# One GNN layer on one core: thirteen blocks of dense work for eight, a gap in the first comparisons, x turned through two banks

## The chip, the cores and the metric

The kernel runs on 1 core of one Trainium2 chip. The metric is the device time of one execution in microseconds, lower is better. Below, PE is TensorE (PEld its weight loads), DVE is VectorE, ACT is ScalarE, POOL is GpSimd and SP is SyncE, whose queue issues most of the DMAs.

## What is computed

A graph with 3125 nodes and 53125 edges sorted by destination, 128 values per node and edge:

```python
msg = x[src] + edge_attr
neigh = segment_sum(msg, dst, num_segments=3125)
rst = (1.0 + eps[0]) * x + neigh
h = rst @ W1 + b1                          # 128 -> 256
h = (h - mean(h, 0)) * rsqrt(var(h, 0) + 1e-5) * gamma + beta
out = relu(h) @ W2 + b2                    # 256 -> 128
y = layernorm(x + out)
```

## The kernel before

The edges are cut into 208 groups of 256. One group is worked on in one window w of the loop in the PE program (L872); window and group order differ. All sums are kept turned, one column of `aggT` per node. Since the edges are sorted by destination, a group touches at most 20 neighbouring nodes.

Every group needs its edge rows summed. `edge_sum` (L837) multiplies the 256 rows, in two halves, with a 0/1 table of 20 columns, in f32; the result goes to one of three banks and DVE adds it into `aggT` (L1214). The rows x[src] come in by one of two ways:

- Gathered groups (50 before). POOL issues two indirect DMAs (L560) that add x[src] to the edge rows already in a slot of `egat`. There are `SLOTS` slots; SP loads a slot's edge rows when the group that used it has been summed (L491).
- Counted groups (158 before, the first 158 in node order). PE counts, with f16 0/1 tables, how often each source node occurs for each of the 20 destinations: `counts_a` (L859, L862) and `counts_b` (L868), 700 columns in all. ACT copies the counts into the f16 matrix `cnt` (L665). DVE makes the tables with comparisons: `hits_k` for two groups at a time (L1125, L1128, L1134), `hits_c` and `hits_g` (L1100) and `hits_n` (L1145). Later the dense work `multiply` (L829) multiplies x with `cnt`.

For the dense work x is split exactly into three bf16 parts, in `xN`, `xr` and `x3` (printed as x_room). `cnt` is cut along the nodes into blocks, `BLOCKS_C` gives the counted groups of each. A block takes 25 tiles of x times 3 parts = 75 units, each a weight load of 128x128 and a matmul whose width is the number of nodes of the block. The widths (`SIZES`) are 120, 180, 256, 376, 468, 466, 332 and 218. The units of block f are spread evenly over the windows between READY[f], when its counts are complete, and READY[f+1] (`share`, L110): the first unit of all is in w = 13, and the last block's 75 units run after the last window. In a counted window, half of the units stand ahead of the first `edge_sum` and half behind `counts_b`; in a gathered window half stand ahead of each `edge_sum`. When a block is done DVE adds it (`add_block`, L1168).

In the windows before and around the first dense unit, called the head here, other work is spread by hand through tables of window numbers:

- SP loads x in seven pieces of 512 nodes in the order of `X_ORDER`: 0, 4, 1, 5, 2, 6, 3. Three are issued ahead of the loop, the others after the windows of `X_AT`.
- `turn_x` turns a piece with four transposes (L773) in a window of `TURN_AT` and ACT scales it into `aggT` (L627). All pieces go through one bank, `ACC`, so a piece waits until the one before it is scaled. The first dense unit waits for all seven.
- The bf16 parts of four pieces are made by DVE (`rest` L1153, `part_3` L1161, windows `SPLITS_W`), those of the other three by PE and ACT: `sum_rest` (L787, L789), windows `RESTS_W`, and `sum_last` (L796) two windows later, through bank `ACC + 1`.
- `fill` (L723) puts matmuls without use ahead of the counts: two for m < 6, one for m < 14.

What of a group goes where is decided when the program is built: `arrange` (L118) walks over the windows with a cost for each and places the gathered groups evenly in that time. PE may be at most three windows ahead of the adds (L877), and DVE makes its tables in the same stream as the adds.

After the last block PE multiplies with W1, DVE takes the statistics, ACT and DVE normalise, PE multiplies with W2 and the rows are normalised and written. The change doesn't touch this part.

Of the kernel before, what the change touches and what calls it, by code (L numbers as in the profile page):

```python
# [5 lines left out]
ALU = mybir.AluOpType  # L6
ACT = mybir.ActivationFunctionType
# [6 lines left out]
P = 128  # L14
BANK = 512
# [5 lines left out]
WIN_A = 12  # L21
FROM_B = 5
WIN_B = 15
GROUPS_C = 158
BLOCKS_C = (10, 12, 17, 25, 31, 31, 22, 10)
CHUNK = 2
CHUNKS = 4
SLOTS = 7
BATCH = 4
BATCHES = 3  # L30
CARRY = 8
# [10 lines left out]
LOADS = 16  # L42
PAD = 8192
PARTS = 3
X_LEAD = 2
SLOTS_W = (0, 2, 5, 7, 10, 13)
SPLITS_W = (3, 6, 10, 14)
RESTS_W = (3, 8, 15)
LATE = 14
BATCHES_G = 2  # L50
KEEP = 0
# [14 lines left out]
FILL_CARRY = 4
FILLS = ((6, 2), (14, 1))
LOAD_0 = 4

def gnn_layer(nc, x, src, dst, edge, eps, w1, b1, gamma, beta, w2, b2, out):
# [6 lines left out]
    NB = -(-N // BANK)  # L78
# [20 lines left out]
    KEYS_A = NT * WIN_A  # L99
# [56 lines left out]
    def width(b):  # L156
        return min(BANK, N - b * BANK)
# [7 lines left out]
    with ExitStack() as ctx:  # L165
# [3 lines left out]
        def sem(name):  # L169
            return ctx.enter_context(nc.semaphore(name))  # L170
# [45 lines left out]
        xN = sb("xN", [P, NT, D])  # L216
# [177 lines left out]
        early_g = columns_of(GC)[0]  # L394
        X_ORDER = [0] + [b for i in range(NB) for b in (early_g + i, 1 + i) if (b < NB if b >= early_g else b == 1 + i)]
        X_ORDER = list(dict.fromkeys(X_ORDER))
        X_AT = [2 + X_LEAD * i for i in range(NB - 3)]
        SLOT_AT = list(SLOTS_W)
        CHUNK_AT = [max(CHUNK * (c - CHUNKS) + CHUNK - 1, min(CHUNK * (c - 2), c + 1)) for c in range(2, GC // CHUNK)]
        W_WEIGHTS = 40  # L400
        assert len(SLOT_AT) == SLOTS - 1 and len(set(CHUNK_AT)) == len(CHUNK_AT)
        SUM_B = [early_g, early_g + 1, early_g - 1]
        SPLIT_B = [b for b in range(NB) if b not in SUM_B]
        SPLIT_AT = list(SPLITS_W)
        REST_AT = list(RESTS_W)
        LAST_AT = [w + 2 for w in REST_AT]
        TURN_AT = [2 * i for i in range(NB)]

        def store_of(w):

# [13 lines left out]
        CLAMP_G = min(GC - GC % LOADS + 3 * LOADS, G)  # L424
        W_CLAMP = 4
        W_CLAMPS = READY[0] + 12
        assert G_AT[0] > 3 and W_CLAMP < G_AT[0] + LAG and W_CLAMPS < min(C_AT[2 * LOADS], G_AT[CLAMP_G - GC])
        W_TESTS = READY[0] + 8
        TEST_F = next(f for f in range(1, F) if READY[f] + 5 > W_TESTS + 8 * TEST_STEP)
        W_WORST = READY[TEST_F] + 5  # L430
# [162 lines left out]
        def _(act):  # L593
# [26 lines left out]
            nc.scalar.activation(carry[:, :].rearrange("p (q h) -> p q h", h=2),  # L620
                                 ps[:, 1, 0:GC].rearrange("p (h q) -> p q h", q=QC), ACT.Copy).then_inc(carry_made, 1)

            def scale_x(i, turned, scaled, bank):

                b = X_ORDER[i]
                act.wait_ge(turned, i + 1)
                nc.scalar.activation(aggT[:, b * BANK:b * BANK + width(b)], bank[:, 0:width(b)], ACT.Copy,  # L627
                                     scale=b2e[:, D:D + 1]).then_inc(scaled, 1)

            def store(made, stored):  # L630
# [8 lines left out]
            for m in range(GC):  # L639
                if m == load_from(m):  # L640
                    act.wait_ge(lows_made, 2 if m < 2 * LOADS else 6)
                    n = load_to(m) - m
                    regs = [act.alloc_register(f"first_act{m + i}") for i in range(n)]
                    act.load(regs, firsts[0:1, m:m + n])
                    lows = [nc.snap(r, donate=True, min_val=0, max_val=CNT - WIN) for r in regs]
                for i in range(len(SUM_B)):
                    t0, t1 = pieces(SUM_B[i])
                    if store_of(REST_AT[i]) == m:
                        act.wait_ge(x_rest_summed, i + 1)
                        nc.scalar.activation(xr[:, t0:t1, :], ps[:, ACC + 1, :].rearrange("p (t d) -> p t d", d=D),  # L650
                                             ACT.Copy).then_inc(x_rest_stored, 1)
                    if store_of(LAST_AT[i]) == m:
                        act.wait_ge(x_last_summed, i + 1)
                        nc.scalar.activation(x3[:, t0:t1, :], ps[:, ACC + 1, :].rearrange("p (t d) -> p t d", d=D),
                                             ACT.Copy).then_inc(x_last_stored, 1)
                for i in range(NB):
                    if store_of(TURN_AT[i]) == m and C_AT[m] > TURN_AT[i]:
                        scale_x(i, x_turned, x_scaled, ps[:, ACC, :])
                act.wait_ge(counts_made, m + 1)
                if m == CORNER:  # L660
                    act.wait_ge(spare_zeroed, 1)
                    act.wait_ge(worst_found, 2)
                if m > 0:
                    act.wait_ge(counts_stored, m)
                nc.scalar.activation(cnt[:, :, bass.ds(lows[m - load_from(m)], WIN)],  # L665
                                     ps[:, m % BANKS_C, 0:KEYS].rearrange("p (t n) -> p t n", n=WIN),
                                     ACT.Copy).then_inc(counts_stored, 1)
                for i in range(NB):
                    if C_AT[m] == TURN_AT[i]:
                        scale_x(i, x_turned, x_scaled, ps[:, ACC, :])  # L670

            act.wait_ge(weights_loaded, 80)
            act.wait_ge(path_known, 1)
# [3 lines left out]
            with act.Else():  # L677
                store(hidden_made, hidden_stored)
                for i in range(NB):
                    scale_x(i, gen_x_turned, gen_x_scaled, ps[:, ACC + i % 2, :])  # L680
                store(gen_hidden_made, gen_hidden_stored)
            act.wait_ge(hidden_moments_made, HH)
            nc.scalar.activation(sd[:, :], bag[:, :, 1], ACT.Sqrt, bias=epsc[:, 0:1]).then_inc(deviation_made, 1)
# [34 lines left out]
        def _(pe):  # L718
# [42 lines left out]
            def turn_x(i, half):  # L761

                b = X_ORDER[i]
                t0, t1 = pieces(b)
                if half == 0:
                    pe.wait_ge(x_loaded[b], 16)
                    pe.wait_ge(key_made, 1)
                    if i > 0:
                        pe.wait_ge(x_scaled, i)
                for t in range(t0 + 2 * half, min(t0 + 2 * half + 2, t1)):  # L770
                    r = rows_of(t)
                    k = (t - t0) * P
                    last = nc.tensor.transpose(ps[:, ACC, k:k + r], xN[0:r, t, :], ident[0:r, 0:r])  # L773
                    if t == t1 - 1:
                        last.then_inc(x_turned, 1)

            def sum_rest(i):

                b = SUM_B[i]
                t0, t1 = pieces(b)  # L780
                pe.wait_ge(x_loaded[b], 16)
                if i == 0:
                    pe.wait_ge(lo_made, 1)
                    pe.wait_ge(minus_made, 1)
                if i > 0:
                    pe.wait_ge(x_last_stored, i)
                nc.tensor.matmul(ps[:, ACC + 1, :], ident[:, :], xN[:, t0:t1, :].rearrange("p t d -> p (t d)"),  # L787
                                 start=True, stop=False, skip_group_check=True)
                nc.tensor.matmul(ps[:, ACC + 1, :].rearrange("p (t d) -> p t d", d=D), minus, upper(xN[:, t0:t1, :]),  # L789
                                 start=False, stop=False, skip_group_check=True).then_inc(x_rest_summed, 1)  # L790
# [212 lines left out]
        def _(dve):  # L1003
# [111 lines left out]
            def hits_k(m):  # L1115

                r = m % RING_K
                if m >= RING_K:
                    dve.wait_ge(counts_made, m - RING_K + 3)

                def pairs(v):
                    return v.rearrange("p (n two) -> p n two", two=2)

                keys = key[:, 2 * m:2 * m + 4, :].rearrange("p (g j) two -> p g j two", j=ROWS)
                nc.vector.tensor_tensor(hit_k[:, r:r + 2, 0:KEYS_A].rearrange("p g (n two) -> p g n two", two=2),  # L1125
                                        pairs(iota_k[:, 0:KEYS_A]).unsqueeze(1).to_broadcast([P, 2, KEYS_A // 2, 2]),
                                        keys[:, :, 0, :].unsqueeze(2).to_broadcast([P, 2, KEYS_A // 2, 2]), ALU.is_equal)
                nc.vector.tensor_tensor(hit_k[:, r:r + 2, KEYS_A:KEYS_A + KEYS_E].rearrange("p g (n two) -> p g n two", two=2),  # L1128
                                        pairs(iota_b[:, :]).unsqueeze(1).to_broadcast([P, 2, KEYS_E // 2, 2]),
                                        keys[:, :, 1, :].unsqueeze(2).to_broadcast([P, 2, KEYS_E // 2, 2]),  # L1130
                                        ALU.is_equal)
                if m == 0:
                    dve.wait_ge(lo_made, 1)
                nc.vector.tensor_tensor(hit_l[:, r:r + 2, :, :].rearrange("p g j (n two) -> p (g j) n two", two=2),  # L1134
                                        pairs(iota_k[:, 0:P]).unsqueeze(1).to_broadcast([P, 2 * ROWS, P // 2, 2]),
                                        lo[:, 2 * m:2 * m + 4, :].unsqueeze(2).to_broadcast([P, 2 * ROWS, P // 2, 2]),
                                        ALU.is_equal).then_inc(key_hits_made, 2)
# [262 lines left out]
```

## Time and profile before

| | |
|---|---|
| median of 3 runs | 258.77 us (257.50 to 259.24) |
| the profiled execution: time | 256.72 us |
| the profiled execution: span of the core | 254.9 us |
| PE busy | 239.1 us (94%), 2147 instructions |
| DVE busy | 182.7 us (72%) |
| POOL busy | 178.7 us (70%) |
| ACT busy | 132.2 us (52%) |

The time holds 1.8 us beside the span. "Busy" is the time in which at least one instruction of the engine ran. PE's matmuls overlap, so its starts tell more than its busy time.

### The profile page before, as it was taken

To read this page: it belongs to the slowest core of one execution; us is meant where nothing else is said; L and a number is where in the kernel's file an instruction comes from. 1 tells how busy PE (TensorE), PEld (TensorE's weight loads), DVE (VectorE), ACT (ScalarE), POOL (GpSimd) and SP (SyncE) were. 2 spreads that over 40 slices of the span, in tenths; PEclk is the share of its full clock that TensorE was granted. 3 is DMA by queue.
4 is the path that set the end of the run, shared out by engine and by line. 5 is a ranking of instruction groups with operands and counts; after the bars stand their busy time and mean duration, and the time that the engine had idled before them with its cause. 6 is when DMAs were issued, how large, how long until landed. Compare 5 with 4: busy or idle time off the path is not lost.

```text
span 254.9 us, 6747 instructions
## 1 busy us (share of the span) xinstructions
PE 239.1 (94%) x2147; PEld 197.8 (78%) x2150; DVE 182.7 (72%) x683; ACT 132.2 (52%) x235; POOL 178.7 (70%) x116
## 2 busy tenths in 40 slices
PE   7997799999999998999999999999999999999970
PEld 3775579989989977888878888888888889645960
DVE  5995757989888867888778687876667311378872
ACT  3365655646556553655554554444443330376793
POOL 4498888888888888888888888888888860550000
PEclk9999999999999999999999999999999999999995
DMA  3868987889988796898787788877756330000044
GB/s 67 236 172 188 230 194 169 186 166 216 208 207 180 193 206 154 194 192 206 180 172 183 191 174 184 180 163 169 169 119 156 74 39 3 0 0 3 3 126 130
DMA packets 51342, 38.13 MB, mean 150 GB/s; under 512 B 5099, under 2 KB 51099, under 8 KB 51305
## 3 DMA queue, kind: packets, MB, share of 16 engines
q1 hardware_dynamic: 36663, 30.89, 43.1%
q0 software_dynamic: 14400, 6.56, 21.5%
q8 instruction: 20, 0.33, 0.6%
q10 hardware_dynamic: 242, 0.21, 0.3%
q14 instruction: 17, 0.14, 0.2%
HBM read 36.05 MB, written 1.60 MB: 148 GB/s over the span
## 4 chain that ended last, share of the span: by engine, by line
PE 83%; DMA 6%; ACT 3%; DVE 3%; issue 2%; POOL 1%; ACTq 1%; another core or an unknown queue 0%; SPq 0%; DVEq 0%; POOLq 0%
PE ps L829 30%; PE ps L837 22%; PE ps L868 11%; PE ps L862 8%; PE ps L806 4%; DMA egat<-in_x_dram,srci 4%; PE ps L948 4%; PE ps L934 2%; PE ps L859 2%; DMA big<-in_src_dram 1%; ACT big L707 1%; DMA egat<-in_edge_attr_dram 1%; ACT big L665 1%; POOL egat L560 1%; ACT aggT L627 1%
## 5 line engine op out<-in xcount | busy, mean ns | idle before, releaser
L560 POOL DMA_INDIRECT egat<-in_x_dram,srci x100 | 168.8, 1688 | 36.4 <-issue 29.0
L665 ACT ACTIVATE big<-ps 128x500 f32 x158 | 96.4, 610 | 92.7 <-PE ps L868 62.7
L837 PEld LDWEIGHTS ps<-hit_c,ebuf 128*128 128x128 f32 x632 | 99.5, 188 | 9.6 <-DVE aggT L1214 2.9
L837 PE MATMUL ps<-hit_c,ebuf 128*128 128x20 f32 x632 | 94.6, 227 | 1.3 <-DVE aggT L1214 1.2
L1214 DVE TENSOR_TENSOR aggT<-aggT,ps 128x20 f32 x208 | 35.9, 173 | 51.1 <-PE ps L837 34.4
L829 PE MATMUL ps<-big,xN 128*128 128x120 f16 (+7 forms) x200 | 58.0, 292 | 1.1 <-ACT aggT L627 0.9
L829 PE MATMUL ps<-big,xr 128*128 128x120 f16 (+7 forms) x200 | 58.0, 292 | 0.0
L829 PE MATMUL ps<-big,x_room 128*128 128x120 f16 (+7 forms) x200 | 57.9, 292 | 0.0
L868 PE MATMUL ps<-hit_k,hit_l 128*128 128x375 f16 x158 | 53.6, 339 | 0.0
L862 PE MATMUL ps<-hit_k,hit_l 128*128 128x300 f16 x158 | 45.5, 288 | 0.0
L1128 DVE TENSOR_TENSOR hit_k<-iota_b,key 128x752 f16<-128x752 f16 x79 | 42.9, 543 | 0.0
L1125 DVE TENSOR_TENSOR hit_k<-iota_k,key 128x600 f16<-128x600 f16 x79 | 36.8, 466 | 0.0
L837 PEld LDWEIGHTS ps<-hit_g,egat 128*128 128x128 f32 x200 | 32.0, 189 | 5.2 <-issue 2.2
L1134 DVE TENSOR_TENSOR hit_l<-iota_k,lo 128x512 f16<-128x512 f16 x79 | 33.0, 417 | 0.0
L837 PE MATMUL ps<-hit_g,egat 128*128 128x20 f32 x200 | 29.5, 229 | 1.7 <-DMA egat<-in_x_dram,srci 1.7
L859 PE MATMUL ps<-hit_n,hit_l 128*128 128x25 f16 x157 | 28.8, 184 | 0.0
L868 PEld LDWEIGHTS ps<-hit_k,hit_l 128*128 128x128 f16 x158 | 28.3, 179 | 0.0
L859 PEld LDWEIGHTS ps<-hit_n,hit_l 128*128 128x128 f16 x157 | 27.3, 174 | 0.7
L829 PEld LDWEIGHTS ps<-big,xN 128*128 128x128 bf16 x200 | 22.2, 111 | 6.7 <-issue 1.7
L829 PEld LDWEIGHTS ps<-big,x_room 128*128 128x128 bf16 x200 | 22.5, 112 | 4.0
L829 PEld LDWEIGHTS ps<-big,xr 128*128 128x128 bf16 x200 | 22.0, 110 | 4.0
L862 PEld LDWEIGHTS ps<-hit_k,hit_l 128*128 128x128 f16 x158 | 15.1, 96 | 0.9
(120 smaller groups left out, 206.5 us busy)
## 6 DMA issues: line engine op xcount, KB each, us to landing
ebuf<-in_edge_attr_dram SPq DMA_DIRECT2D x79, 256.0 KB
egat<-in_edge_attr_dram SPq DMA_DIRECT2D x49, 128.0 KB
egat<-in_x_dram,srci POOLq DMA_INDIRECT x100
xN<-in_x_dram SPq DMA_DIRECT2D x6, 256.0 KB, 4.3
out_dram<-big SPq DMA_DIRECT2D x5, 256.0 KB
w_sb<-in_L_gnn_W_dram SPq DMA_DIRECT2D x2, 128.0 KB
out_dram<-big SPq DMA_DIRECT2D x2, 128.0 KB
big<-in_src_dram ACTq DMA_DIRECT2D x1, 192.0 KB
```

The lines of the kernel that those rows point to most:

```text
L560: return nc.gpsimd.indirect_dma_start(to, None, x[:, :], bass.IndirectOffsetOnAxis(ap=ix, axis=0), compute_op=op)
L665: nc.scalar.activation(cnt[:, :, bass.ds(lows[m - load_from(m)], WIN)], ps[:, m % BANKS_C, 0:KEYS].rearrange("p (t n) -> p t n", n=WIN), A ...
L806: nc.tensor.matmul(ps[:, n % BANKS_C, 0:width(b)], w1_sb[:, h * P:(h + 1) * P], aggT[:, b * BANK:b * BANK + width(b)], start=True, stop=Tr ...
L829: last = nc.tensor.matmul(ps[:, ACC + f % 2, 0:SIZES[f]], part_v, cnt[:, t, STARTS[f]:STARTS[f] + SIZES[f]], start=(u == 0), stop=(u == UN ...
L837: last = nc.tensor.matmul(ps[:, SUMS + w % BANKS_S, 0:WIN], rows_v[:, j * D:(j + 1) * D], hits_v, start=(j == 0), stop=(j == ROWS - 1))
L859: nc.tensor.matmul(counted(m)[:, :, 0], hit_l[:, (m - 1) % RING_K, 1, :], hit_n[:, (m - 1) // CARRY % 2, (m - 1) % CARRY, :], start=True, ...
L862: nc.tensor.matmul(counted(m)[:, :, 0:WIN_A], hit_l[:, m % RING_K, 0, :], hit_k[:, m % RING_K, 0:KEYS_A].rearrange("p (t n) -> p t n", n=W ...
L868: nc.tensor.matmul(counted(m)[:, :, FROM_B:WIN], hit_l[:, m % RING_K, 1, :], hit_k[:, m % RING_K, KEYS_A:KEYS_A + KEYS_B].rearrange("p (t ...
L1125: nc.vector.tensor_tensor(hit_k[:, r:r + 2, 0:KEYS_A].rearrange("p g (n two) -> p g n two", two=2), pairs(iota_k[:, 0:KEYS_A]).unsqueeze(1 ...
L1128: nc.vector.tensor_tensor(hit_k[:, r:r + 2, KEYS_A:KEYS_A + KEYS_E].rearrange("p g (n two) -> p g n two", two=2), pairs(iota_b[:, :]).unsq ...
L1134: nc.vector.tensor_tensor(hit_l[:, r:r + 2, :, :].rearrange("p g j (n two) -> p (g j) n two", two=2), pairs(iota_k[:, 0:P]).unsqueeze(1).t ...
L1214: nc.vector.tensor_tensor(to, to, ps[:, SUMS + v % BANKS_S, 0:WIN], ALU.add).then_inc(window_added, 1)
```

## The change

There are 13 blocks in place of 8, with widths 120, 150, 166, 180, 182, 196, 194, 212, 210, 212, 210, 196 and 218. So there are 975 units in place of 600, the last 75 as before at the width 218 behind the last window. 160 groups are counted and 48 gathered. There are six slots for gathered rows in place of seven. x is turned alternately through the banks `ACC` and `ACC + 1`, in windows that follow more closely, and its pieces are loaded one window earlier or more. `sum_rest` starts later and takes the pieces in the order 3, 4, 5. DVE's `rest` moves by two or three windows. The fillers end at m = 10. In the first seven `hits_k`, the second comparison waits for the first one's semaphore.

```diff
-GROUPS_C = 158
-BLOCKS_C = (10, 12, 17, 25, 31, 31, 22, 10)
+GROUPS_C = 160
+BLOCKS_C = (10, 10, 11, 12, 12, 13, 13, 14, 14, 14, 14, 13, 10)
...
-SLOTS = 7
+SLOTS = 6
...
-SLOTS_W = (0, 2, 5, 7, 10, 13)
-SPLITS_W = (3, 6, 10, 14)
-RESTS_W = (3, 8, 15)
+SLOTS_W = (0, 2, 5, 7, 10)
+SPLITS_W = (5, 8, 12, 17)
+RESTS_W = (9, 12, 15)
+TURNS_W = (0, 2, 3, 5, 7, 8, 10)
+PORT = 14
...
-HITS = 3200
+HITS = 3000
...
-GATHER_FIRST = 19000
+GATHER_FIRST = 18000
...
-FILLS = ((6, 2), (14, 1))
+FILLS = ((4, 2), (10, 1))
...
-        X_AT = [2 + X_LEAD * i for i in range(NB - 3)]
+        X_AT = [1 + X_LEAD * i for i in range(NB - 3)]
...
-        SUM_B = [early_g, early_g + 1, early_g - 1]
+        SUM_B = [early_g - 1, early_g, early_g + 1]
...
-        TURN_AT = [2 * i for i in range(NB)]
+        TURN_AT = list(TURNS_W)
+        BEFORE_SUMS = max(i for i in range(NB) if i % 2 == 1) + 1
...
                 if half == 0:
                     pe.wait_ge(x_loaded[b], 16)
-                    pe.wait_ge(key_made, 1)
-                    if i > 0:
-                        pe.wait_ge(x_scaled, i)
+                    if i == 0:
+                        pe.wait_ge(key_made, 1)
+                    if i == 1:
+                        pe.wait_ge(lo_made, 1)
+                    if i > 1:
+                        pe.wait_ge(x_scaled, i - 1)
...
-                    last = nc.tensor.transpose(ps[:, ACC, k:k + r], xN[0:r, t, :], ident[0:r, 0:r])
+                    last = nc.tensor.transpose(ps[:, ACC + i % 2, k:k + r], xN[0:r, t, :], ident[0:r, 0:r])
...
                 if i == 0:
-                    pe.wait_ge(lo_made, 1)
                     pe.wait_ge(minus_made, 1)
+                    pe.wait_ge(x_scaled, BEFORE_SUMS)
...
-                                        keys[:, :, 0, :].unsqueeze(2).to_broadcast([P, 2, KEYS_A // 2, 2]), ALU.is_equal)
+                                        keys[:, :, 0, :].unsqueeze(2).to_broadcast([P, 2, KEYS_A // 2, 2]),
+                                        ALU.is_equal).then_inc(first_keys_made, 1)
+                if m < PORT:
+                    dve.wait_ge(first_keys_made, m // 2 + 1)
```

The next two pieces are PE's instructions in one counted window of the middle of the program, and the start of the one behind it, before and after. The names before the arrow are the bank tensor, those behind it the operands; the last number is the width.

Before, in the block of width 466:

```order
L837 MATMUL ps<-hit_c,ebuf 128x20 [waits window_added]
L859 MATMUL ps<-hit_n,hit_l 128x25 [waits key_hits_made,counts_stored]
L862 MATMUL ps<-hit_k,hit_l 128x25x12
L837 MATMUL ps<-hit_c,ebuf 128x20
L868 MATMUL ps<-hit_k,hit_l 128x25x15
L829 MATMUL ps<-big,xr 128x466
L829 MATMUL ps<-big,x_room 128x466
L837 MATMUL ps<-hit_c,ebuf 128x20 [waits chunk_loaded0,chunk_hits_made,window_added]
```

After, in the block of width 194:

```order
L844 MATMUL ps<-hit_c,ebuf 128x20 [waits window_added]
L866 MATMUL ps<-hit_n,hit_l 128x25 [waits key_hits_made,counts_stored]
L869 MATMUL ps<-hit_k,hit_l 128x25x12
L844 MATMUL ps<-hit_c,ebuf 128x20
L875 MATMUL ps<-hit_k,hit_l 128x25x15
L836 MATMUL ps<-big,xr 128x194
L836 MATMUL ps<-big,x_room 128x194
L836 MATMUL ps<-big,xN 128x194
L836 MATMUL ps<-big,xr 128x194
L844 MATMUL ps<-hit_c,ebuf 128x20 [waits chunk_loaded3,window_added]
```

Two wide units became four narrow ones, and the edge sum behind them follows a narrow matmul instead of a wide one.

The first `sum_rest` stood in w = 3 and took piece 4, which three windows of waiting work had long brought in:

```order
L837 MATMUL ps<-hit_c,ebuf 128x20 [waits window_added]
L787 MATMUL ps<-xN,ident 128x512 [waits minus_made,lo_made,x_loaded4]
L789 MATMUL ps<-xN,big 128x512
L723 MATMUL ps<-iota_b 128x375 [waits counts_stored]
L723 MATMUL ps<-iota_b 128x375
```

After the change it stands in w = 9, one window behind that of w = 8 (the first two rows), and takes piece 3:

```order
L844 MATMUL ps<-hit_c,ebuf 128x20 [waits window_added]
L780 MATMUL ps<-ident,xN 128x53 [waits x_scaled,x_loaded6]
...
L844 MATMUL ps<-hit_c,ebuf 128x20 [waits chunk_loaded0,chunk_hits_made,window_added]
L794 MATMUL ps<-xN,ident 128x512 [waits x_scaled,minus_made,x_loaded3]
L796 MATMUL ps<-xN,big 128x512
L727 MATMUL ps<-iota_b 128x375 [waits counts_stored]
L866 MATMUL ps<-hit_n,hit_l 128x25 [waits key_hits_made]
```

Piece 3 is the last in `X_ORDER`; SP issues it after the sum of w = 7.

## Rows read from the trace of the kernel before

**Rows 1.** The page: engines' busy time, and the clock in 40 slices.

```profile
PE 239.1 (94%) x2147; PEld 197.8 (78%) x2150; DVE 182.7 (72%) x683; ACT 132.2 (52%) x235; POOL 178.7 (70%) x116
...
PEclk9999999999999999999999999999999999999995
```

**Rows 2.** Two stretches: busy PE, PEld, DVE, ACT, POOL (x count), clock, DMA share, GB/s.

```profile
10.40:31.50 21.10, 16.70 (x132) 13.24 (x133) 17.13 (x55) 12.32 (x22) 18.36 (x10) 1.00 0.82 203
31.50:211.40 179.90, 178.36 (x1753) 152.90 (x1754) 132.97 (x499) 91.20 (x150) 149.67 (x91) 1.00 0.77 172
```

**Rows 3.** Timeline of PE in the head: start, duration, instruction, [idle before it <-releaser].

```profile
15.35 1.10 PE L787 MATMUL ps<-xN,ident 128*128 128x512 f32 x2
...
21.79 0.37 PE L837 MATMUL ps<-hit_g,egat 128*128 128x20 f32 x2 [1.74 <-DMA egat<-in_x_dram,srci]
...
27.49 0.23 PE L773 MATMUL ps<-ident,xN 53*128 53x53 f32 x1 [0.85 <-ACT aggT L627]
...
31.41 0.21 PE L829 MATMUL ps<-big,xN 128*128 128x120 f16 x1 [0.87 <-ACT aggT L627]
```

**Rows 4.** Timeline of POOL, second gather; and the group of all gathers.

```profile
11.58 5.71 POOL L560 DMA_INDIRECT egat<-in_x_dram,srci  x1 [0.30 <-issue]
...
L560 POOL DMA_INDIRECT egat<-in_x_dram,srci x100 | 168.8, 1688 | 36.4 <-issue 29.0 <-DMA egat<-in_edge_attr_dram 7.4
```

**Rows 5.** Timeline of DVE in the head.

```profile
14.29 0.46 DVE L1125 TENSOR_TENSOR hit_k<-iota_k,key 128x600 f16<-128x600 f16 x1
14.68 0.54 DVE L1128 TENSOR_TENSOR hit_k<-iota_b,key 128x752 f16<-128x752 f16 x1
...
19.53 0.17 DVE L1214 TENSOR_TENSOR aggT<-aggT,ps 128x20 f32 x1 [0.26 <-issue]
```

**Rows 6.** Timeline: issue of the last piece of x, and the transpose waiting for it.

```profile
25.65 0.38 SPq L452 DMA_DIRECT2D xN<-in_x_dram  x1
...
29.70 0.20 PEld L773 LDWEIGHTS ps<-ident,xN 128*128 128x128 f32 x2 [0.22 <-DMA xN<-in_x_dram]
```

**Rows 7.** Timeline of PE: a counted window with five units of width 120.

```profile
45.54 0.35 PE L837 MATMUL ps<-hit_c,ebuf 128*128 128x20 f32 x2
45.74 0.18 PE L859 MATMUL ps<-hit_n,hit_l 128*128 128x25 f16 x1
...
46.46 0.35 PE L837 MATMUL ps<-hit_c,ebuf 128*128 128x20 f32 x2
```

**Rows 8.** Timeline of PE: a counted window with three units of width 180.

```profile
49.87 0.33 PE L837 MATMUL ps<-hit_c,ebuf 128*128 128x20 f32 x2
50.04 0.18 PE L859 MATMUL ps<-hit_n,hit_l 128*128 128x25 f16 x1
...
50.74 0.33 PE L837 MATMUL ps<-hit_c,ebuf 128*128 128x20 f32 x2
```

**Rows 9.** Timeline of PE: a counted window with two units of width 468.

```profile
143.46 0.29 PE L837 MATMUL ps<-hit_c,ebuf 128*128 128x20 f32 x2
143.59 0.18 PE L859 MATMUL ps<-hit_n,hit_l 128*128 128x25 f16 x1
...
144.26 0.36 PE L829 MATMUL ps<-big,xr 128*128 128x468 f16 x1
144.46 0.29 PE L837 MATMUL ps<-hit_c,ebuf 128*128 128x20 f32 x2
```

**Rows 10.** The chain that ended last: start, us, units in a row (width 376, 332, 218).

```profile
110.25 0.32 PE ps L829 x2
...
200.06 0.70 PE ps L829 x5
...
212.11 7.01 PE ps L829 x75
```

**Rows 11.** Timeline of PE: two of the stalls behind DVE's adds.

```profile
52.99 0.40 PE L837 MATMUL ps<-hit_c,ebuf 128*128 128x20 f32 x2 [0.56 <-DVE aggT L1214]
...
96.28 0.40 PE L837 MATMUL ps<-hit_c,ebuf 128*128 128x20 f32 x2 [0.68 <-DVE aggT L1214]
```

More of the change, by code:

```diff
@@ L315, in gnn_layer @@
         slot_hits_made = sem("slot_hits_made")
+        first_keys_made = sem("first_keys_made")
         key_hits_made = sem("key_hits_made")
@@ L426, in gnn_layer @@
         W_CLAMPS = READY[0] + 12
-        assert G_AT[0] > 3 and W_CLAMP < G_AT[0] + LAG and W_CLAMPS < min(C_AT[2 * LOADS], G_AT[CLAMP_G - GC])
+        assert G_AT[0] > 3 and W_CLAMP < G_AT[0] + LAG and W_CLAMPS < min(C_AT[2 * LOADS], (G_AT + [G])[CLAMP_G - GC])
         W_TESTS = READY[0] + 8
@@ L621, in _, with scale_x @@
                                  ps[:, 1, 0:GC].rearrange("p (h q) -> p q h", q=QC), ACT.Copy).then_inc(carry_made, 1)
-            def scale_x(i, turned, scaled, bank):
+            def scale_x(i, turned, scaled):
                 b = X_ORDER[i]
                 act.wait_ge(turned, i + 1)
-                nc.scalar.activation(aggT[:, b * BANK:b * BANK + width(b)], bank[:, 0:width(b)], ACT.Copy,
+                nc.scalar.activation(aggT[:, b * BANK:b * BANK + width(b)], ps[:, ACC + i % 2, 0:width(b)], ACT.Copy,
                                      scale=b2e[:, D:D + 1]).then_inc(scaled, 1)
@@ L657, in _ @@
                     if store_of(TURN_AT[i]) == m and C_AT[m] > TURN_AT[i]:
-                        scale_x(i, x_turned, x_scaled, ps[:, ACC, :])
+                        scale_x(i, x_turned, x_scaled)
                 act.wait_ge(counts_made, m + 1)
@@ L669, in _ @@
                     if C_AT[m] == TURN_AT[i]:
-                        scale_x(i, x_turned, x_scaled, ps[:, ACC, :])
+                        scale_x(i, x_turned, x_scaled)
             act.wait_ge(weights_loaded, 80)
@@ L679, in _ @@
                 for i in range(NB):
-                    scale_x(i, gen_x_turned, gen_x_scaled, ps[:, ACC + i % 2, :])
+                    scale_x(i, gen_x_turned, gen_x_scaled)
                 store(gen_hidden_made, gen_hidden_stored)
```

## The prediction

> **What bounds the kernel now.** The page comes first: PE is busy for 94% of the span and its clock stays at its upper level, 2.4 GHz, until the last slice [rows 1]. But PE's matmuls overlap, so a busy share does not prove that PE sets the pace. For that I read the busy time by stretch [rows 2] and then the timeline of PE, where an idle time has its releaser behind it. Two parts differ.
>
> In the windows from 13 on (31.5 to 211.4 us) DVE has 133.0 of 179.9 us, POOL 149.7, ACT 91.2, and PE is issuing nearly throughout. A counted window takes the same time wherever it stands, but for its units and what the unit's width does to the instruction behind it [rows 7 to 9]. So here PE is the bound, and the time is a sum of instruction steps. In the head (10.4 to 31.5 us) 13 windows take 21.1 us, 1.6 us each, with PE busy for 16.7 [rows 2]; there waits decide: 1.74 us for the first gathered rows, 0.85 and 0.87 us for ACT's scaling of x [rows 3].
>
> **The dense work, width by width.** A unit's step is the time from its start to the next instruction's. Five units of 120 and the window's other work take 46.46 - 45.54 = 0.92 us [rows 7]; three of 180, 0.87 [rows 8]; two of 468, 1.00, one step of 468 being 0.20 [rows 9]. Steps in a row: 0.16 at 376, 0.70/5 = 0.140 at 332, 7.01/75 = 0.0935 at 218 [rows 10]. At 2.4 GHz 218 columns are 90.8 ns, so 2.6 ns are lost there; 332 loses 2, 376 and 468 4 to 8. At 120 and 180 I put 53.4 and 79 ns (3.4 and 4 over the columns). Before: 75 x (53.4 + 79 + 113 + 165 + 203 + 200 + 141) ns = 71.6 us ahead of the last block; 113 for 256 columns, 165 and 200 are taken between these rows. After: the twelve widths have 2228 columns, /2.4 = 928 ns, plus 12 x 3.5 ns = 970, x 75 = 72.8 us. So 375 more units cost **+1.2 us**, between +0.4 (2.6 ns per unit) and +2.1 (4.5 ns). The last block is the same 75 x 218 in both.
>
> The Trainium skill (TensorE: Matmul & The Clock Gate, Back-to-back issue gap) speaks harder against narrow units: streams of weight load and matmul are said to hold about 81 ns per pair at 128 columns. Five steps of 120 in this trace fit in 0.26 us, so the trace does not agree; by the page's figure, as an estimate with the line between its 81 ns (128) and 131 ns (512), 900 units near 90 ns would make 81 us, 8 us more than I sum.
>
> **What follows a narrow unit.** Take the units out of a window. At 468: 1.00 - 2 x 0.20 = 0.60 us. At 180: 0.87 - 3 x 0.079 = 0.633. At 120: 0.92 - 5 x 0.0534 = 0.655. The difference is seen in one place: from the edge sum behind the units (L837) to L859 it is 0.13 us behind width 468, 0.17 behind 180, 0.20 behind 120 [rows 7 to 9]. Before, only the two first blocks (windows 13 to 50) pay it; after, every window does. Widths 194 to 212 give 84 to 92 ns of cover, so 0.02 to 0.03 us stay in a counted window. A gathered window has units ahead of both sums and pays twice; without them it is 0.27 us at wide units, 0.34 at 180, 0.39 at 120 by the same count.
>
> Windows 13 to 206, outside the units. Before 148 counted, 46 gathered: 13 x 0.66 + 17 x 0.637 + 118 x 0.60 = 90.2, gathered 3 x 0.39 + 5 x 0.34 + 38 x 0.272 = 13.2, together 103.4 us. After 149 and 45: counted 9 x 0.66 + 11 x 0.648 + 13 x 0.641 + 25 x 0.636 + 91 x 0.626 = 94.3, gathered 4 x 0.39 + 13 x 0.349 + 28 x 0.32 = 15.1, together 109.4. That is **+6.0 us** (4.5 to 6.5), of which 0.3 is the one more counted window. Extras: one `sum_rest` (1.1 us [rows 3] and its window's rest) stays behind w = 13 in both; a `sum_last` of 0.2 us more, four fillers of 0.157 (375 columns) less: 2.0 before, 1.6 after, **-0.4**.
>
> 71.6 + 103.4 + 2.0 = 177.0 us against 179.9 on the trace: 2.9 us are stalls, such as 0.56 and 0.68 us behind DVE's adds [rows 11]. They come where DVE has registers to load, a block to add or tests to make while PE's windows are short (0.9 us). The new windows there are nearer 1.0, though there are five more blocks to add. I take 1.1 us after, **-1.8** (0 to -2.9). Sum from 13 on: 1.2 + 6.0 - 0.4 - 1.8 = **+5.0 us**.
>
> **The head.** PE's own work in it hardly changes. Before: 10 counted windows x 0.61, 3 gathered x 0.38, 16 fillers x 0.157, six turns x 0.44 and a small one, two `sum_rest` x 1.17, two `sum_last` x 0.22: 15.3 us of 21.1. After: 11, 2, 14, the same turns, two and one: 15.0. So only waits can go, 5.8 us in all.
>
> - The gap. The second gather took 5.71 us against a mean of 1.69 [rows 4], while DVE's comparisons ran without a break: 14.68 starts before 14.29 + 0.46 has ended [rows 5]. With a gap in each of seven `hits_k` the gather should end some 4 us earlier, and the 1.74 us go. Cost on DVE: the start slips from 0.08 before the end to some 0.04 behind it, 7 x 0.12 = 0.8 us.
> - What is late next. PE may open w = 7 only when the sum of w = 4 is added. DVE did that at 19.53 [rows 5] and will again: it loses a `rest` of 0.68 us there and gains the gaps. So w = 7 opens at 19.6 instead of 22.65, w = 9 at about 21.7 (0.77 us per window, 0.44 for four transposes).
> - Then piece 3. SP issues it after the sum of w = 7, at about 20.4. Before, that piece took from 25.65 to 29.70, 4.0 us [rows 6]; so it lands at 24.4, and `sum_rest` in w = 9 waits some **2.6 us**. Behind it PE's queue stands, and with it the counts for ACT and the chunks' release. Then 1.1 + 0.8 (w = 9), 0.8 (w = 10, gathered with a turn), 1.0 (w = 11), 2.0 (w = 12 with the second `sum_rest`): w = 13 opens at 30.0 instead of 31.5. The 0.87 us ahead of the first unit are gone, since the last turn is in w = 10.
>
> **-1.5 us**, from -4.5 (landing within 2.7 us, adds in time) to +1.5 (landing late, DVE behind).
>
> Two gathered groups fewer save POOL 4 x 1.99 us (1.69 and 0.30 idle [rows 4]), and six slots reach over 26 windows; gathered rows were awaited only once [rows 3], so both cost and gain nothing. The end behind 211.4 us is untouched.
>
> **Sum.** +5.0 - 1.5 = +3.5 us. The profiled execution took 256.72 (span 254.9 and 1.8 outside), so 260.2; it was 2.05 us below the median of 258.77, and on the median it is **262.3 us**. A measurement here tells about 1% (2.6 us) from no change.
>
> **Rivals.**
>
> 1. *The step behind the units belongs to the time, not the width* (faster). If the 0.17 and 0.20 us come from the loaded DMA queues of the first 66 us, all windows behind are 0.60 and 0.27: 149 x 0.60 + 45 x 0.272 = 101.6, so 72.8 + 101.6 + 1.6 + 1.1 = 177.1 from window 13 on, -2.8, with the head -4.3: 254.5 us. It decides once the step from L837 to L859 at widths 182 to 212 is under 0.14. Against it: the step changes with the width, by the same count in each block.
> 2. *The head gives all it can.* Piece 3 lands in time: w = 13 at 26.5, -5.0, and the total is 0: 258.8 us.
> 3. *The gap does not free POOL.* The first rows land at 21.65 again, w = 9 opens at 25, piece 3 still comes late: head +1, total +6: 264.8 us. In the Trainium skill (SBUF — State Buffer) a DVE operation on two SBUF inputs holds off only GpSimd's reads, and descriptor writing is inferred to be free of it; by that alone the gap would do nothing. The 5.71 us row speaks against it.
> 4. *The clock falls.* An idle time of 2.6 us in w = 9 with fewer fillers lets PE's clock fall to 1.2 GHz; 4 us of work doubled is +4: 266 us. The 1.74 us idle did not do it (clock 1.00 in rows 2).
>
> **Chances.** Forecast 0.52, rival 1 0.12, rival 2 0.18, rival 3 0.12, rival 4 0.06. The forecast's own range is 260 to 265 from its terms, and a quarter of it is within 1%: same = 0.18 + 0.13 = 0.31, slower = 0.39 + 0.12 + 0.06 = 0.57, faster 0.12. The range 257.2 to 266.0 leaves out rival 1 and the far ends.
>
> **What would show it.** Right: the second gather under 2.5 us; an idle of 2 to 3 us ahead of L794 in w = 9, released by the DMA of x; the first unit at 29 to 31 us; L844 to L866 0.155 to 0.165 us at widths 194 to 212; last window 183 to 186 us behind w = 13; a tail of 43.5 us. Wrong: windows of 0.60 us beside their units, a clock under 1.00, or stalls of over 3 us behind L1224.

## The result, and the profile after

The changed kernel takes 262.18 us (median of 20 runs, 259.90 to 265.69), the kernel before 259.67 us (20 runs, 254.95 to 262.00). The ratio is 1.0144, with a 95% interval of 1.0105 to 1.0183: slower by some 1%. This ratio, like all below, leaves out executions more than 1.5% above the fastest of their kernel (here 5 of the changed kernel's 20), so it is not the ratio of the two medians, which is 1.0097. An execution's time and its mean PE clock go together, and this makes most of the spread: the changed kernel's six executions of 259.9 to 260.3 us have clocks of 0.989 to 0.994, its five longest 0.968 to 0.970.

I forecast a ratio of 262.3/258.77 = 1.014 as the sum of +5.0 us behind window 13 and -1.5 us in the head. The profiled execution (span 259.8 us) shows the first term nearly as forecast and the second one not. Its time is 262.10 us, 2.3 us more than its span, where the kernel before has 1.8 us; the forecast had no term for this.

The page of the changed kernel, against [rows 1]: PE, weight loads, DVE, ACT and POOL busy, the clock by slices, and the group of the gathers.

```profile
PE 247.2 (95%) x2525; PEld 217.4 (84%) x2525; DVE 185.5 (71%) x690; ACT 133.3 (51%) x237; POOL 166.4 (64%) x112
...
PEclk9996899999999999999999999999999999999995
...
L564 POOL DMA_INDIRECT egat<-in_x_dram,srci x96 | 156.6, 1631 | 42.2 <-issue 27.1
```

PE and its weight loads are busier, POOL has 12 us less to do. The new thing is the 6 and the 8 in the clock row. The stretches show it better (columns as in [rows 2]: duration, busy PE, PEld, DVE, ACT, POOL, clock, DMA share, GB/s):

```profile
9.90:21.60 11.70, 10.34 (x86) 8.25 (x87) 11.01 (x34) 6.01 (x11) 9.38 (x6) 1.00 0.94 244
21.60:28.40 6.80, 5.93 (x23) 3.81 (x22) 3.18 (x11) 2.54 (x5) 5.48 (x4) 0.50 0.73 174
28.40:32.10 3.70, 3.68 (x30) 2.64 (x29) 3.19 (x10) 2.62 (x5) 1.91 (x2) 1.00 0.60 140
32.10:216.20 184.10, 184.01 (x2128) 171.48 (x2127) 135.75 (x509) 93.19 (x154) 139.51 (x86) 1.00 0.75 166
```

From 21.6 to 28.4 us PE ran at 1.2 GHz. The windows from 13 on take 184.1 us against 179.9, with PE busy in all but 0.1. What follows them takes 43.5 us in both.

The timeline of PE at width 212, against [rows 7 to 9]:

```profile
180.14 0.25 PE L836 MATMUL ps<-big,x_room 128*128 128x212 f16 x1
180.23 0.31 PE L844 MATMUL ps<-hit_c,ebuf 128*128 128x20 f32 x2
180.39 0.18 PE L866 MATMUL ps<-hit_n,hit_l 128*128 128x25 f16 x1
...
181.22 0.32 PE L844 MATMUL ps<-hit_g,egat 128*128 128x20 f32 x2
```

The edge sum's step to L866 is 0.16 us where it was 0.13 behind width 468 in [rows 9] and 0.14 in the median of all windows from width 256 up, and the window is 0.99 us with four units of 0.0925: 0.62 outside them.

The head, on POOL against [rows 4], and on PE against [rows 3]:

```profile
9.62 2.05 POOL L564 DMA_INDIRECT egat<-in_x_dram,srci  x1 [6.20 <-DMA egat<-in_edge_attr_dram]
11.97 1.78 POOL L564 DMA_INDIRECT egat<-in_x_dram,srci  x1 [0.30 <-issue]
```

```profile
18.23 0.62 PE L844 MATMUL ps<-hit_g,egat 128*128 128x20 f32 x4
19.42 0.40 PE L844 MATMUL ps<-hit_c,ebuf 128*128 128x20 f32 x2 [0.57 <-DVE aggT L1224]
20.41 0.44 PE L780 MATMUL ps<-ident,xN 128*128 128x128 f32 x2 [0.59 <-DMA xN<-in_x_dram]
...
24.75 2.05 PE L794 MATMUL ps<-xN,ident 128*128 128x512 f32 x2 [0.80 <-ACT aggT L631]
26.59 0.64 PE L796 MATMUL ps<-xN,big 128*128 128x512 bf16 x1
```

The second gather takes 1.78 us in place of 5.71 and nothing waits for gathered rows. Window 7 opens at 19.42 us (22.65 before), behind an add of DVE. Then PE waits for pieces of x and for ACT, the clock falls, L794 takes 2.05 us in place of 1.10, and window 13 opens at 32.2 us, 0.7 later than before.

In a_8blocks below, whose head has the same instructions, the clock stays at 2.4 GHz there. The same wait is longer then, its releaser is the DMA of x alone, and window 13 opens at 30.4 us:

```profile
24.81 1.12 PE L794 MATMUL ps<-xN,ident 128*128 128x512 f32 x2 [1.48 <-DMA xN<-in_x_dram]
```

### The profile page after: what moved, and what is told of

It is laid out like the page before. It is cut to its first block, busy times and chain, and to the rows that moved or that the text cites. A ratio compares the mean times of both kernels' runs of the same rounds, so it can differ in the third digit from the quotient of the medians.

```text
span 259.8 us, 7518 instructions
## 1 busy us (share of the span) xinstructions
PE 247.2 (95%) x2525; PEld 217.4 (84%) x2525; DVE 185.5 (71%) x690; ACT 133.3 (51%) x237; POOL 166.4 (64%) x112
## 3 DMA queue, kind: packets, MB, share of 16 engines
q0 software_dynamic: 13824, 6.30, 20.2%
## 4 chain that ended last, share of the span: by engine, by line
PE 88%; DMA 4%; DVE 2%; ACT 2%; issue 1%; ACTq 0%; SPq 0%; DVEq 0%
PE ps L836 30%; PE ps L844 23%; PE ps L875 11%; PE ps L869 8%; PE ps L813 4%; PE ps L955 4%; DMA xN<-in_x_dram 3%; PE ps L941 2%; PE ps L866 2%; PE ps L794 2%; ACT big L711 1%; DMA big<-in_src_dram 1%; PE ps L780 1%; PE ps L727 1%; DVE big L1355 0%
## 5 line engine op out<-in xcount | busy, mean ns | idle before, releaser
L564 POOL DMA_INDIRECT egat<-in_x_dram,srci x96 | 156.6, 1631 | 42.2 <-issue 27.1
L844 PE MATMUL ps<-hit_c,ebuf 128*128 128x20 f32 x640 | 99.0, 233 | 0.7 <-DVE aggT L1224 0.6
L836 PE MATMUL ps<-big,xr 128*128 128x196 f16 (+9 forms) x325 | 78.5, 244 | 0.0
L836 PE MATMUL ps<-big,xN 128*128 128x196 f16 (+9 forms) x325 | 78.5, 245 | 0.0
L836 PE MATMUL ps<-big,x_room 128*128 128x196 f16 (+9 forms) x325 | 78.4, 244 | 0.0
L836 PEld LDWEIGHTS ps<-big,xr 128*128 128x128 bf16 x325 | 34.5, 106 | 3.9
L836 PEld LDWEIGHTS ps<-big,xN 128*128 128x128 bf16 x325 | 34.3, 106 | 3.9
L836 PEld LDWEIGHTS ps<-big,x_room 128*128 128x128 bf16 x325 | 33.8, 104 | 3.6
L866 PE MATMUL ps<-hit_n,hit_l 128*128 128x25 f16 x159 | 29.4, 185 | 0.0
L866 PEld LDWEIGHTS ps<-hit_n,hit_l 128*128 128x128 f16 x159 | 27.8, 175 | 1.3 <-issue 0.9
L875 PEld LDWEIGHTS ps<-hit_k,hit_l 128*128 128x128 f16 x160 | 28.8, 180 | 0.0
L579 POOL TENSOR_TENSOR xN<-xN,b2e 128x3200 f32<-128x3200 f32 x1 | 7.0, 6963 | 22.1 <-issue 22.1
```

Of the source, the lines that this page charges most:

```text
L564: return nc.gpsimd.indirect_dma_start(to, None, x[:, :], bass.IndirectOffsetOnAxis(ap=ix, axis=0), compute_op=op)
L836: last = nc.tensor.matmul(ps[:, ACC + f % 2, 0:SIZES[f]], part_v, cnt[:, t, STARTS[f]:STARTS[f] + SIZES[f]], start=(u == 0), stop=(u == UN ...
L844: last = nc.tensor.matmul(ps[:, SUMS + w % BANKS_S, 0:WIN], rows_v[:, j * D:(j + 1) * D], hits_v, start=(j == 0), stop=(j == ROWS - 1))
L866: nc.tensor.matmul(counted(m)[:, :, 0], hit_l[:, (m - 1) % RING_K, 1, :], hit_n[:, (m - 1) // CARRY % 2, (m - 1) % CARRY, :], start=True, ...
L875: nc.tensor.matmul(counted(m)[:, :, FROM_B:WIN], hit_l[:, m % RING_K, 1, :], hit_k[:, m % RING_K, KEYS_A:KEYS_A + KEYS_B].rearrange("p (t ...
```

## The experiments

The ratios are to runs of the kernel before on the same chip; their medians there were 258.9 to 259.2 us. "Head" is the time from the first edge sum to the opening of window 13, and the next column goes on from there to the opening of the last window, 207; in parentheses stands how much of it ran at 1.2 GHz. The profile is one execution of each.

| kernel | head | windows 13 to 207 | span | lowest, median of runs |
|---|---|---|---|---|
| before | 21.1 (0) | 179.9 | 254.9 | 254.95, 259.67 |
| changed | 22.2 (6.8) | 184.1 | 259.8 | 259.90, 262.18 |
| b_13blocks | 22.7 (3.4) | 183.6 | 259.9 | 260.52, 263.31 |
| a_8blocks | 20.1 (0) | 182.6 (3.4) | 256.4 | 258.33, 258.69 |
| a_edges_late | 20.0 (0) | 180.0 | 253.6 | 255.60, 258.25 |
| b_edges_late | 26.2 (6.8) | 179.4 | 259.0 | 255.75, 258.67 |
| a_nogap | 22.8 (6.8) | 184.1 | 260.6 | 262.85, 265.38 |
| b_gap | 20.2 (0) | 179.6 | 253.7 | 254.83, 255.42 |
| a_rests_late | 19.2 (0) | 186.0 | 258.6 | one run, 260.86 |
| combo13 | 18.8 (0) | 182.2 | 254.8 | 256.56, 259.67 |
| b_gap_edges | 20.8 (0) | 180.8 (3.4) | 255.5 | 255.06, 255.32 |
| a_edges_fills | 22.5 (3.4) | 180.5 | 256.6 | 256.49, 257.47 |

### The blocks, both ways

b_13blocks, the kernel before with narrow blocks:

```diff
-BLOCKS_C = (10, 12, 17, 25, 31, 31, 22, 10)
+BLOCKS_C = (10, 10, 11, 12, 12, 13, 13, 14, 14, 14, 13, 12, 10)
```

> Only the blocks of the kernel before are cut anew, 13 in place of 8 (158 counted groups, everything else untouched). By my theory (a narrow unit does not cover the f32 weights of the edge sum behind it) the windows from 13 on take 4 to 5 us more than the 179.9 us of before, the step from the edge sum to the carry matmul is 0.155 to 0.165 us behind widths 194 to 212 against 0.13 behind 468, and the time is 3 to 6 us above before. By the rival (the blocks cost nothing, the head does) the time stays within 1 us of before.

Measured: the windows from 13 on take 183.6 us, +3.8, just under the 4 to 5 expected. 263.31 us is the median of four runs and 260.52 the lowest, against 258.90 and 255.24 us of the kernel before beside them: 4 to 5 us more, in the 3 to 6 expected. The step behind width 194 is 0.17 us:

```profile
129.85 0.32 PE L837 MATMUL ps<-hit_c,ebuf 128*128 128x20 f32 x2
130.02 0.18 PE L859 MATMUL ps<-hit_n,hit_l 128*128 128x25 f16 x1
```

The rival (the blocks cost nothing, the head does) is out: the blocks alone cost as much as the whole change.

a_8blocks, the changed kernel with wide blocks:

```diff
-BLOCKS_C = (10, 10, 11, 12, 12, 13, 13, 14, 14, 14, 14, 13, 10)
+BLOCKS_C = (10, 12, 17, 25, 32, 32, 22, 10)
```

> The changed kernel with eight wide blocks again (10, 12, 17, 25, 32, 32, 22, 10), the rest of the change kept. By my theory the windows from 13 on fall by 4 to 5 us from 184.1 us, to 179 to 181, and the time comes to within 2 us of before. By the rival it stays at the changed kernel's 1.4% above before.

Measured: 258.69 us (median of four runs), 3.5 us under the changed kernel and level with the 258.90 us of before beside it. The ratio to before, 1.0126 (1.0028 to 1.0224), does not tell it from the changed kernel: all four executions had mean clocks of 0.973 to 0.987. The decision rests on the windows. The windows from 13 on take 182.6 us, above the 179 to 181 I named. PE's clock fell in the middle of this execution, behind two waits for DVE:

```profile
93.47 0.40 PE L844 MATMUL ps<-hit_g,egat 128*128 128x20 f32 x2 [0.41 <-DVE aggT L1224]
95.01 0.40 PE L844 MATMUL ps<-hit_c,ebuf 128*128 128x20 f32 x2 [0.68 <-DVE aggT L1224]
```

```profile
95.00:99.00 4.00, 3.99 (x24) 3.40 (x25) 3.19 (x12) 1.22 (x2) 3.31 (x3) 0.57 0.63 132
```

Of 3.4 us at half speed some 1.7 us are lost; without them it would be 180.9, as expected (an estimate). So wide blocks have a price too: waits for DVE's adds. One of them, of 0.68 us at 96.3 us in the kernel before [rows 11], comes behind a load of registers that holds DVE's queue for 1.11 us from 93.19 us on. That short windows bring these waits about is argued, not shown. Waits of this kind were 2.9 us before and are 0.6 to 0.7 us in both kernels with thirteen blocks.

### Whether it is the covering of weight loads

a_edges_late keeps every block, and moves both edge sums of a counted window behind a wide count:

```diff
-                edge_sum(w, 0, rows_v, hits[:, h, :])
+                late = w in C_OF and w > READY[0]
+                if not late:
+                    edge_sum(w, 0, rows_v, hits[:, h, :])
...
+                if late:
+                    edge_sum(w, 0, rows_v, hits[:, h, :])
+                    counts_b(C_OF[w])
                 edge_sum(w, 1, rows_v, hits[:, h + 1, :])
                 if w in TURN_AT:
                     turn_x(TURN_AT.index(w), 1)
+                if w in C_OF and not late:
+                    counts_b(C_OF[w])
                 if w in C_OF:
-                    counts_b(C_OF[w])
```

> The changed kernel, but in the counted windows behind the first block's start the first edge sum stands behind the 300-column count and the second behind the 375-column count, so both have a wide matmul ahead of them; blocks and widths are kept. If uncovered weight loads are the cost, a counted window's rest falls from 0.62 to 0.63 us to 0.60 or less at the same widths, 149 windows x 0.02 to 0.03 = 3 to 4.5 us less. If the loss belongs to the narrow units themselves or to the time in the program, the window stays the same and the step only moves to another instruction.

Measured: 180.0 us in place of 184.1, **-4.1 us** with the same 975 units; median 258.25 us of ten runs, ratio to before 1.0017 (0.9954 to 1.0081), so the loss of the change is gone. Its timeline at width 212:

```profile
181.07 0.25 PE L836 MATMUL ps<-big,xN 128*128 128x212 f16 x1
181.16 0.19 PE L866 MATMUL ps<-hit_n,hit_l 128*128 128x25 f16 x1
181.19 0.29 PE L869 MATMUL ps<-hit_k,hit_l 128*128 128x300 f16 x1
181.32 0.29 PE L844 MATMUL ps<-hit_c,ebuf 128*128 128x20 f32 x2
181.46 0.34 PE L875 MATMUL ps<-hit_k,hit_l 128*128 128x375 f16 x1
181.63 0.30 PE L844 MATMUL ps<-hit_c,ebuf 128*128 128x20 f32 x2
181.77 0.25 PE L836 MATMUL ps<-big,xr 128*128 128x212 f16 x1
...
182.13 0.19 PE L866 MATMUL ps<-hit_n,hit_l 128*128 128x25 f16 x1
```

Both edge sums take 0.14 us now, and the window with four units takes 0.97 us against 0.99. Outside its units a counted window now takes 0.605 to 0.608 us at every width (medians), where it took 0.660 at 120, 0.635 at 180 and 0.620 at 212. The gathered windows, whose edge sums still stand behind narrow units, kept their steps in the same run: 0.198 us behind 120, 0.173 behind 180, 0.161 behind 212. The loss does not belong to narrow units as such, but to the f32 edge sums that follow them.

The sizes say that it is the load of their weights. In the changed kernel the step of the edge sum exceeds the 0.140 us of the wide blocks by 58, 34, 26 and 20 ns behind units whose own steps are 52, 77, 84 and 91 ns (widths 120, 180, 196 and 212): 110 to 111 ns together each time. So some 111 ns have to be covered, and behind width 256 (109 ns) the excess is 1 to 2 ns. This is the 110 ns of cover that the prediction named.

The units gained too: the mean of what their step has over the columns fell from 3.5 to 2.1 ns, stalls left out, 1.2 us in all. That comes from one unit in each counted window, the one directly behind the count of 375 columns (97 ns, the others 91, at width 212 in the changed kernel):

```profile
180.85 0.26 PE L836 MATMUL ps<-big,xN 128*128 128x212 f16 x1
180.95 0.25 PE L836 MATMUL ps<-big,xr 128*128 128x212 f16 x1
181.04 0.25 PE L836 MATMUL ps<-big,x_room 128*128 128x212 f16 x1
```

Now an edge sum stands there and takes 0.145 us in place of 0.138, so the 7 ns only moved.

b_edges_late is the same edit in the kernel before.

> The same order of edge sums in the kernel before. By my theory only the windows of the blocks of width 120 and 180 gain (30 counted windows x 0.035 to 0.06 = 1.3 us), the wide ones nothing; the time is 0 to 1.5 us below before. If the order itself costs something (the adds come later in the window), it shows here as a wide window over 0.60 us.

Measured: 179.4 us, 0.5 less than before, where I had named 1.3. The unit behind the count gained there too (376 columns: from 165 to 158 ns, 1.2 us over all units), but the counted windows are now 0.606 to 0.608 us outside their units at every width, 0.006 over the 0.600 of the wide blocks: the same 7 ns, moved to the edge sum. The ratio is 1.0048 (0.9989 to 1.0106), no difference: the order pays where units are narrow.

Its head of 26.2 us has another reason, which belongs to the next section. The first gather took 9.72 us, and PE waited for its rows:

```profile
9.77 9.72 POOL L560 DMA_INDIRECT egat<-in_x_dram,srci  x1 [6.36 <-DMA egat<-in_edge_attr_dram]
23.96 0.58 PE L837 MATMUL ps<-hit_g,egat 128*128 128x20 f32 x2 [3.85 <-DMA egat<-in_x_dram,srci]
```

### The gap

a_nogap takes the gap out of the changed kernel (`PORT = 0`), b_gap puts it alone into the kernel before:

```diff
-                                        keys[:, :, 0, :].unsqueeze(2).to_broadcast([P, 2, KEYS_A // 2, 2]), ALU.is_equal)
+                                        keys[:, :, 0, :].unsqueeze(2).to_broadcast([P, 2, KEYS_A // 2, 2]),
+                                        ALU.is_equal).then_inc(first_keys_made, 1)
+                if m < 14:
+                    dve.wait_ge(first_keys_made, m // 2 + 1)
```

> The changed kernel without the wait between the first two comparisons. By my theory POOL's second gather takes 5 to 6 us again in place of 1.8, the first gathered rows land at about 21 us, window 7 opens at 21.5 to 22.5 in place of 19.4 and piece 3 of x is asked for that much later: window 13 opens 1.5 to 3 us later than with the gap. If the gap does nothing, the second gather is short without it too and all stays.

> The gap alone in the kernel before. By my theory the second gather takes 1.8 us, the wait of 1.74 us for the first gathered rows goes, window 7 opens at 19.5 to 20.5 in place of 22.65, and the head shortens by 1 to 2.5 us, the rest taken back by the pieces of x. If the gap does nothing, the second gather stays at 5 to 6 us.

The timeline of POOL without the gap in the changed kernel, then with it in the kernel before:

```profile
9.62 6.03 POOL L564 DMA_INDIRECT egat<-in_x_dram,srci  x1 [6.21 <-DMA egat<-in_edge_attr_dram]
15.96 1.69 POOL L564 DMA_INDIRECT egat<-in_x_dram,srci  x1 [0.30 <-issue]
```

```profile
9.68 2.24 POOL L561 DMA_INDIRECT egat<-in_x_dram,srci  x1 [6.26 <-DMA egat<-in_edge_attr_dram]
12.22 1.79 POOL L561 DMA_INDIRECT egat<-in_x_dram,srci  x1 [0.30 <-issue]
```

Without the gap one gather of the first two takes 6 us; this time the first, not the second as I had written. With it, 2.2 and 1.8. All twelve profiles agree: in the four kernels without the gap one of the first two gathers takes 5.71 to 9.72 us, in the eight with it none takes over 2.24. So DVE's unbroken run of comparisons of two SBUF inputs at the start does hold up the issue of an indirect DMA, by 4 us and more. It does not do so everywhere: behind the start gathers take 1.5 to 2.0 us beside the same comparisons without a gap, and what makes the difference stays open. The Trainium skill (SBUF — State Buffer, Who interferes with whom) infers that `tensor_tensor` leaves descriptor generation free; these runs say otherwise.

b_gap takes 255.42 us (ten runs), ratio **0.9888** (0.9855 to 0.9921): faster than both kernels of the case. Its head is 0.9 us shorter in the profile, just under the 1 to 2.5 I named. Window 7 opened at 21.59 us, not at 19.5 to 20.5: the 1.74 us for gathered rows are gone, but window 7 now waits 0.75 us for the edge rows of its counted chunk. The median gains 3.8 us against the runs beside it, more than the head alone: six of its ten executions have a mean clock of 0.990 or more, of the nineteen of before beside it two. Why the gap should keep the clock up is not shown. a_nogap has 265.38 us, 1.0266 of before (1.0185 to 1.0348), where the changed kernel has 1.0144. Its window 7 opens at 22.1 us, as expected. Window 13 opens at 33.0 us, 0.8 later than in the changed kernel's profile and 2.6 later than where the clock did not fall. But its clock falls twice in the head (12.3 to 15.7 and 22.5 to 25.9 us), and it waited 1.11 us for the first x, so its head is no clean measure of the gap.

The head of the changed kernel in its undisturbed executions (20.1 us in a_8blocks, which has it unchanged) equals b_gap's 20.2. So the two banks, the closer turns and the earlier loads of x together show no gain on top of the gap.

### The wait in window 9

a_rests_late: `RESTS_W = (11, 14, 17)` in place of (9, 12, 15).

> The changed kernel with the three sum_rest in windows 11, 14 and 17 in place of 9, 12 and 15, so that the first no longer stands ahead of the loading of piece 3 and the scaling of piece 6. If this wait of window 9 is what the head of the changed kernel still loses, window 9 takes 0.8 us in place of 3.5 to 4.7, and window 13 opens about 2.5 us earlier, at 27.5 to 28.5 us; the clock does not fall in the head. If the loads of x pace the head, the wait only moves to the turn in window 10.

Measured: window 9 takes 0.8 us, and the wait moved to the turn in window 10, as the second reading said:

```profile
19.66 0.40 PE L844 MATMUL ps<-hit_c,ebuf 128*128 128x20 f32 x2 [0.56 <-DVE aggT L1224]
20.62 0.44 PE L780 MATMUL ps<-ident,xN 128*128 128x128 f32 x2 [0.56 <-DMA xN<-in_x_dram]
25.09 0.44 PE L780 MATMUL ps<-ident,xN 128*128 128x128 f32 x2 [1.19 <-DMA xN<-in_x_dram]
```

Window 13 opens at 29.4 us, 1 us earlier than in the undisturbed changed head, not 2.5. The `sum_rest` and the `sum_last` that left the head cost 1.9 us more behind window 13 (186.0). DMA carries 240 GB/s in this head against 203 in [rows 2], and two of its waits end with a load of x. That the loads pace it is read from these waits, not tested apart.

combo13 joins this with a_edges_late.

> Thirteen blocks, the edge sums of counted windows behind the wide counts, and the sum_rest in windows 11, 14 and 17. If both effects are what I take them for, they add: window 13 opens at 27.5 to 28.5 us, the windows from 13 on take 180 us, and the span is 251 to 252 us, 3 us under before; the time 253 to 255 us. If the head's gain is lost to DVE or ACT behind it, the span stays at 253 to 254.

Measured: the head is 18.8 us, but the windows from 13 on take 182.2 us, 2.2 more than in a_edges_late; span 254.8 and not 251 to 252, ratio 1.0000 (0.9932 to 1.0068). The effects don't add: what leaves the head is paid behind it, in part with new waits for DVE's adds ahead of L794 (0.32 and 0.27 us).

### Two more versions

> The kernel before with the gap and with the edge sums behind the wide counts. Against the gap alone (span 253.7 us, 1.1% under before) the order gave 0.5 us in the windows from 13 on; if both add, the span is 253 us and the time 0.985 to 0.99 of before. If the later edge sums make PE wait for DVE's adds in the head's wake, it stays at 0.99 or above.

b_gap_edges (gap and late edge sums in the kernel before) takes 255.32 us (seven runs), ratio **0.9848** (0.9812 to 0.9884): the best of the case, though its interval overlaps that of the gap alone. In its profiled execution the clock fell from 31.5 to 34.9 us, so its span of 255.5 is no measure of it; the other six have spans of 253.1 to 253.6 us, as expected.

> Thirteen blocks with the edge sums behind the wide counts and the fillers of the kernel before (20 in place of 14). If the missing fillers let PE's clock fall in the head in part of the executions, the spread shrinks: mean clock 0.985 to 0.995 in all of them in place of 0.964 to 0.991, best time 0.5 to 1 us above the 255.6 us without fillers, median 1 to 2 us below the 258.25. If waits and not fillers decide, the spread stays as it is.

a_edges_fills (a_edges_late with `FILLS = ((6, 2), (14, 1))`): median 257.47 us, ratio 0.9934 (0.9899 to 0.9970). The lowest run is 0.9 us dearer than without the fillers, the highest 258.98 in place of 261.56. The lowest mean clock rises from 0.964 to 0.975, not to the 0.985 I named: half of the runs still fell below 0.988, the profiled one at 26.4 us. So the fillers don't prevent the fall. That they narrow the spread is not shown, since these ten runs were on another chip, where the kernel before spread over 3.2 us in place of 6.9 too.

## Why the prediction was right, and where not

- **PE as the bound behind window 13**: right. Terms forecast and measured there: units 72.8, 73.1 us; other work and extras 111.0, 110.4 with the 1.1 for the stalls apart; stalls 1.1, 0.6. The sum +5.0, measured +4.2: units +1.5, other work and extras some +5.0 where +5.6 was forecast, stalls -2.3.
- **The units, +1.2 us**: +1.5. The excess over the columns was 3.2 to 3.7 ns by width, stalls left out, against the 3.5 taken. The 81 ns of the Trainium skill's page for streams of weight load and matmul (TensorE: Matmul & The Clock Gate, Back-to-back issue gap) don't hold here: widths 120 to 150 took 53 to 66 ns.
- **The uncovered weight load, +6.0 us**: right in place and size, 0.619 to 0.630 us at widths 194 to 212 against the 0.626 taken. That the cost hangs on the width of what stands ahead of an f32 edge sum was argued then and is now shown by a_edges_late; that it is the load of the weights rests on the 111 ns that come out at every width. Rival 1 (time, not width) is out. The 0.13 us read behind width 468 was one row; the median is 0.14.
- **Stalls, -1.8**: -2.3, in the direction and nearly the size forecast.
- **The head, -1.5 us**: wrong in sum, +1.1 in the profiled execution. The gap did what was forecast (1.78 us, window 7 at 19.4 against 19.6 said); rival 3 is out. Window 9 opened at 23.5 in place of 21.7 (at 23.0 where the clock did not fall): the turns of windows 7 and 8 waited for their own pieces of x, a wait that I had not put in. It also made SP issue piece 3 at 21.3 in place of 20.4. The first `sum_rest` waited until 24.75; the load of piece 3 and ACT's scaling of piece 6 ended within 0.1 us of each other. Where the clock did not fall, it waited 1.3 to 1.5 us for the load alone, as forecast in kind, where 2.6 was named. So rival 2, a piece 3 in time, is out as well.
- **The failed step** is "the clock falls", priced as a rival at 0.06, and one of the prediction's own signs of being wrong (a clock under 1.00). Without the fall the same head takes 20.1 us, -1.0, close to the forecast. With it, 6.8 us ran at half speed. It is no rival but a part of many executions of both kernels (of the 19 of the kernel before beside a_8blocks, the nine longest have mean clocks of 0.977 to 0.979, the shortest six 0.990 to 0.995); what brings it down is open. The forecast was built on the one profile of the kernel before, and between the two profiled executions the difference in time is +5.4 us, not +3.5: head +1.1 for -1.5, windows +4.2 for +5.0, an earlier start -0.4 and 0.5 outside the span that had no term. That the median came within 0.2 us of the 262.3 named is partly luck: the medians of 20 runs are 2.5 us apart, and the kernel before lay 0.9 us above its median of three.
- **Two gathered groups fewer, six slots**: nothing, as said; no wait for gathered rows from window 6 on.

## What to carry to other kernels

Before cutting a matmul narrower, look at what stands behind it: a narrow matmul may cost a few nanoseconds itself and twenty or thirty more in the next instruction, whose weights it no longer covers. The same cut cost next to nothing (180.0 us against 179.9) once the f32 weight loads of the counted windows stood behind wide matmuls. And gaps of some 0.04 us in a solid run of DVE operations can free GpSimd for microseconds, which here was worth more than all rearranging around it.

## What the runs showed that I had not expected

- The granted clock fell to 1.2 GHz with PE busy most of the time: from 21.6 us in the changed kernel, behind waits of 0.57 and 0.59 us (5.93 of the next 6.8 us busy), at 95.3 us in a_8blocks behind waits of 0.41 and 0.68 us, while 1.74 us in one piece did not bring it down in the profile of before. In b_edges_late it fell within the wait of 3.85 us, at 23.3 us.
- Whatever stands directly behind the count of 375 columns takes 7 ns more: a unit of 376 columns 165 ns in place of 158, an edge sum 145 in place of 138. It moved with the order of the instructions in a_edges_late and b_edges_late. Why is open.
- The starved gather was the first of the two in a_nogap, b_13blocks and b_edges_late (6.03, 5.97 and 9.72 us) and the second in the kernel before (5.71). Which of them is caught is not set by the program: b_13blocks and the kernel before are the same up to there.
